# Cross attention and a sorted mixture of experts on one core: first masks in six pieces, tails cleared earlier and in larger blocks, fewer waits for landings

## The reference, cut to what matters

```python
# x (16, 100, 128), ctx (16, 1444, 128), mask (16, 1444)
x = x + tanh(g_xattn) * xattn(layernorm(x), ctx, mask)      # one head, softmax over 1444 keys
#   att = q . w_input + (q * dot_scale) @ ctx.T - 1e30 * mask ; softmax(att) @ ctx
x = x + tanh(g_ffn) * moe(layernorm(x))                      # 8 experts, top 2 of 8
#   per token and expert: W_down @ (silu(W_gate @ t) * (W_up @ t)), F = 512, weighted by the gates
```

## Time and profile before

| what | value |
|---|---|
| runs before | 282.87 us median of 3 (278.66, 322.13, 282.87) |
| profiled execution | 280.85 us, span 278.8 us, mean granted clock 0.946 |
| PE busy | 242.4 us of 278.8 (87%) |
| DVE, ACT, POOL busy | 144.4, 137.0, 112.2 us |
| attention, 16 batches | from 12.4 us to about 152 us |
| first expert tile / tile 8 / last down | gate and up at 148.2 / 184.5 / 257.7 us |
| last reads, additions and stores | 262.7 to 278 us |

### The profile page before, as it was taken

One profiled execution on the slowest core, in us unless ns is written; L12 is line 12 of the kernel. 1 busy time (PEld: TensorE's weight loads), 2 busy tenths in 40 slices (PEclk: granted clock), 3 DMA queues, 4 the chain that ended last, 5 costly groups with the idle time before them and its releaser, 6 DMA issues.

```text
span 278.8 us, 5798 instructions
## 1 busy us (share of the span) xinstructions
PE 242.4 (87%) x1614; PEld 198.3 (71%) x1615; DVE 144.4 (52%) x467; ACT 137.0 (49%) x302; POOL 112.2 (40%) x197
## 2 busy tenths in 40 slices
PE   6799999999999999999978599699999999998100
PEld 6557777788777788777778387588888888887100
DVE  3434666767777767787746338223433343432024
ACT  3445455676555686655545234345545555545000
POOL 3250432157644476636374535433424223233200
PEclk9989999999999999999979979989999999999855
DMA  5875787778787888888632003221211111000164
GB/s 134 223 199 149 186 218 195 187 210 228 200 244 210 214 191 207 206 218 225 246 76 49 15 2 91 63 70 58 58 39 45 54 38 38 28 19 31 34 218 119
DMA packets 17645, 36.49 MB, mean 131 GB/s; under 512 B 3692, under 2 KB 9460, under 8 KB 17620
## 3 DMA queue, kind: packets, MB, share of 16 engines
q1 hardware_dynamic: 13580, 31.36, 43.4%
q0 software_dynamic: 2560, 3.77, 4.5%
q10 hardware_dynamic: 1480, 1.05, 1.2%
HBM read 30.89 MB, written 5.27 MB: 130 GB/s over the span
## 4 chain that ended last, share of the span: by engine, by line
PE 70%; DMA 8%; issue 6%; DVE 5%; ACT 4%; POOL 4%; SPq 0%; POOLq 0%; DVEq 0%; ACTq 0%
PE psum L1067 14%; PE psum L1046 13%; PE psum L1170 9%; PE psum L1022 7%; PE psum L1148 6%; PE psum L1150 5%; PE psum L1149 5%; PE psum L1159 4%; DMA ctx_sb<-results 3%; PE psum L1057 2%; DMA slots<-pair_rows,slot_i 2%; ACT probsT L616 2%; POOL slots L527 2%; DMA results<-y_sb,dest 2%; ACT qT L611 1%
## 5 line engine op out<-in xcount | busy, mean ns | idle before, releaser
L583 POOL DMA_INDIRECT results<-y_sb,dest x32 | 30.7, 959 | 57.1 <-DVE dest L948 25.6
L1067 PE MATMUL psum<-ctx_sb,probsT 120*100 120x128 f32 (+1 forms) x384 | 49.2, 280 | 0.0
L959 DVE SCALAR_TENSOR_TENSOR scores<-probs,row_in,psum 128x512 f32<-128x512 f32 x32 | 23.9, 747 | 42.6 <-ACT probs L691 41.3
L1067 PEld LDWEIGHTS psum<-ctx_sb,probsT 120*100 120x100 f32 (+1 forms) x384 | 44.9, 172 | 0.3 <-issue 0.2
L1046 PE MATMUL psum<-ctxT,qT 128*100 128x512 f32 (+1 forms) x96 | 43.2, 587 | 0.0
L527 POOL DMA_INDIRECT slots<-pair_rows,slot_i x32 | 33.5, 1046 | 22.6 <-DVE slot_i L846 8.4
L691 ACT ACTIVATE probs<-psum 128x512 f32<-128x512 f32 x32 | 19.1, 598 | 39.0 <-PE psum L1150 39.0
L1170 PE MATMUL psum<-w_down,hidT 128*128 x256 | 34.3, 277 | 0.8 <-ACT y_sb L706 0.6
L782 DVE CUSTOM_DVE_ANT_0 scores<-psum,maskb 100x1444 f32<-100x1444 f32 x16 | 26.6, 1660 | 13.3 <-PE psum L1046 13.3
L1170 PEld LDWEIGHTS psum<-w_down,hidT 128*128 128x128 f32 x256 | 31.5, 194 | 1.2 <-issue 1.2
L1148 PE MATMUL psum<-w_hi,rowT_hi 128*128 x64 | 29.1, 454 | 2.4 <-issue 1.0
(11 more groups left out here) (138 smaller groups left out, 372.2 us busy)
## 6 DMA issues: line engine op xcount, KB each, us to landing
ctx_sb<-in_ctx SPq DMA_DIRECT2D x16, 720.0 KB
maskb<-mask_scaled SPq DMA_DIRECT2D x14, 564.1 KB
w_raw<-in_w_experts SPq DMA_DIRECT2D x16, 256.0 KB, 6.0
row_in<-slots SPq DMA_DIRECT2D x32, 65.0 KB, 1.9
w_down<-in_w_experts SPq DMA_DIRECT2D x4, 512.0 KB, 9.2
ctx_sb<-results SPq DMA_DIRECT2D x4, 200.0 KB
ctx_sb<-results ACTq DMA_DIRECT2D x4, 200.0 KB
out<-x_all SPq DMA_DIRECT2D x4, 200.0 KB
```

The costliest lines, as they stand in the source:

```text
L583: nc.gpsimd.indirect_dma_start(results, bass.IndirectOffsetOnAxis(ap=dest[:, s:s + 1], axis=0), y_sb[:, s, :], None).then_inc(y_stored[s], 16)
L1067: last = nc.tensor.matmul(attn_ps[0:Q, 0:D], probsT[0:rows[c], c, :], ctx_sb[0:rows[c], b % RING, c, :], start=(c == 0), stop=(c == CHUNKS ...
```

## The change

The changes, by place:

- **First masks.** The mask is padded to 1536 keys and laid as 48 pieces of 512. One transfer brings the first 32 pieces and a second one pieces 0 to 5 again, into rows 32 to 37; one ACT instruction of 38 x 512 and one DVE instruction of 6 x 512 take the place of the 16 x 1444 ones. `add_mask` is three matmuls, not six, and that of batch 0 moves ahead of `transpose_q(0)`. The scaling and the storing of the masks move behind the eviction of the first context, and `load_ctx(3)` behind the wait for that store. Tanh moves behind the first exponential. Seven of the 17 filler matmuls go (`keep_warm`: 10, 3 and 4 become 10 and 2, with the third call gone).
- **Attention.** `transpose_q(b+1)` and `copy_qT(b+1)` move behind the transposed context, PE's behind the first third of `attend`, ACT's ahead of the exponential.
- **End of attention.** The routing of batch 13 moves out of `step(15)` to behind it; orders on PE, ACT and DVE change for the last three batches; `transpose_rows(8)` moves to the end of step 7; the late tables are spread over tiles 3 to 6 on DVE.
- **Tails.** `tail_row` is written in `place(6)`, when 14 batches are counted. SP clears 328 rows behind that point for each of the 8 experts, each with one transfer of 82 partitions x 4 rows (82 x 2080 bytes). SP's row load of tile 8 does not wait for them; instead POOL waits for all of them before it scatters batches 14 and 15.
- **Waits of POOL.** Late scatters are `scatter(11)`, root2(14), wait, `scatter(12)`, root2(15), `scatter(13)`, last gates, wait for tails, `scatter(14)`, `scatter(15)`. `scatter_result` waits for no landing.

```diff
+TAIL_ROWS = 328
+TAIL_PART = 82
-        empty = sb("empty", [P, ROW])
+        empty = sb("empty", [P, SPREAD, ROW])          # SPREAD = TAIL_ROWS // TAIL_PART = 4
...
             load_x(0)
-            sp.dma_start(mask_rows, mask).then_inc(mask_raw, 16)
+            sp.dma_start(first_raw[0:LOW, :], pieces[0:LOW, :]).then_inc(first_loaded_mask, 16)
+            sp.dma_start(first_raw[LOW:first_rows, :], pieces[0:MASKED * PIECES, :]).then_inc(first_loaded_mask, 16)
             load_ctx(0)
             load_x(1)
+            sp.dma_start(mask_rows, mask[:, 0:K]).then_inc(mask_raw, 16)
             load_ctx(1)
...
                 if k == EARLY:
                     sp.wait_ge(late_ready, 1)
-                    sp.wait_ge(tails_stored, 16 * E)
                     sp.wait_ge(empty_stored, 16)
                     sp.wait_ge(scattered[1], 16 * 2 * (B - PARTS[EARLY_PART][1]))
...
             def clear_tail(e):
-                at = sp.value_load(tail_row[0:1, e:e + 1], min_val=0, max_val=DUMMY)
-                sp.dma_start(slots[bass.ds(at, P), :], empty[:, :]).then_inc(tails_stored, 16)
+                at = sp.value_load(tail_row[0:1, e:e + 1], min_val=0, max_val=DUMMY - TAIL_ROWS)
+                sp.dma_start(slots[bass.ds(at, TAIL_ROWS), :].rearrange("(p r) d -> p r d", r=SPREAD),
+                             empty[0:TAIL_PART, :, :]).then_inc(tails_stored, 16)
...
                 if n == EARLY - 1:
                     sp.wait_ge(tails_ready, 1)
-                    for e in range(SP_TAILS):
+                    for e in range(E):
                         clear_tail(e)
...
-            pair_landed(1)
-            scatter(12)
+            scatter(11)
             root2(B - 2)
             normalise2(B - 2)
             pair_landed(1)
-            scatter(13)
+            scatter(12)
             root2(B - 1)
             normalise2(B - 1)
+            scatter(13)
             last_gates()
-            pair_landed(1)
+            pool.wait_ge(tails_stored, 16 * E)
             scatter(14)
-            pair_landed(1)
             scatter(15)
-            pair_landed(1)
...
                 pool.wait_ge(dest_done, n + 1)
-                if k % 2 == 0:
-                    wait(pool, y_stored[(k - 1) % YRING], i * 16 + 16 * ((k + YRING - 1) // YRING) if k else 0)
                 apart(pool)
...
             def step(b):                                # ACT
-                if 0 <= b - 1 < B:
-                    if b + 1 < B:
-                        act.wait_ge(probsT_raw, (b - 1) * GROUPS + 1)
-                        copy_qT(b + 1)
+                if b >= 1:
                     for g in range(GROUPS):
                         copy_probsT(b - 1, g)
...
-                if 0 <= b - 2 < B - 2:
+                if 0 <= b - 2 < B - 3:
                     copy_xn2T(b - 2)
+                if b + 1 < B:
+                    copy_qT(b + 1)
...
                 dve.wait_ge(rank_raw, p + 1)            # DVE, place(p)
+                if p == LAST - 1:
+                    nc.vector.tensor_copy(tail_row[:, :], at[:, N, :]).then_inc(tails_ready, 1)
                 if p == LAST:
-                    nc.vector.tensor_copy(tail_row[:, :], at[:, N, :]).then_inc(tails_ready, 1)
...
             def between(n):                             # DVE, after tile n
                 if n == 3:
+                    tile_counts(True)
+                if n == 4:
                     tile_runs(True)
-                if n == 4:
-                    tile_tables(True)
+                if n == 5:
+                    tile_experts(True)
+                if n == 6:
+                    tile_rows(True)
...
-                for n in range(0, K, 512):              # PE, add_mask(b)
-                    m = min(512, K - n)
-                    nc.tensor.matmul(scores_ps[0:Q, n:n + m], select[:, b, :], mask_hi[:, n:n + m], start=True, stop=False)
-                    nc.tensor.matmul(scores_ps[0:Q, n:n + m], select[:, b, :], mask_lo[:, n:n + m], start=False, stop=False)
+                for t, n in enumerate(range(0, K, PIECE)):
+                    m = min(PIECE, K - n)
+                    nc.tensor.matmul(scores_ps[0:Q, n:n + m], select[:, b * PIECES + t, :], first_split[:, 0:m], start=True, stop=False)
...
-                if b == 0:                              # PE, step(b)
-                    keep_warm(4)
                 if 4 <= b and b % 2 == 0:
                     ranks((b - 4) // 2)
...
+                if 2 <= b < B - 1:
+                    transpose_xn2(b - 2)
+                if b >= 1:
                     attend(b - 1, 0, 1)
+                if b + 1 < B:
+                    transpose_q(b + 1)
...
-                if 0 < k and k + 1 < T:                 # PE, tile_step
+                if 0 < k and k + 1 < T and k != EARLY - 1:
                     transpose_rows(i, k + 1)
...
+                if k == EARLY - 1:
+                    transpose_rows(i, k + 1)
                 if k == 2:
+                    route(B - 1)
                     pe.wait_ge(x2_done, B)
                     pe.wait_ge(down_loaded, 16 * 4)
```

More of the change, by code:

```diff
@@ L78, in build @@
     CUTS = 4
+    PIECES = 3
+    PIECE = mask.shape[1] // PIECES
+    LOW = 32
+    assert PIECE == 512 and K <= PIECES * PIECE and MASKED * PIECES <= LOW
+    SPREAD = TAIL_ROWS // TAIL_PART
+    assert TAIL_ROWS >= (TOKENS - PARTS[-2][1] * Q) + P - 1 and PARTS[-2][1] * Q + TAIL_ROWS <= REGION
     CUT = B // CUTS
@@ L366, in _ @@
             load_ctx(2)
-            load_ctx(RING - 1)
             sp.wait_ge(mask_stored, 16)
             load_mask(MASKED)
+            load_ctx(RING - 1)
             load_x(3)
@@ L381, in _ @@
                     sp.wait_ge(empty_done, 1)
-                    sp.dma_start(slots[DUMMY:DUMMY + P, :], empty[:, :]).then_inc(empty_stored, 16)
+                    sp.dma_start(slots[DUMMY:DUMMY + P, :], empty[:, 0, :]).then_inc(empty_stored, 16)
             for m in range(4):
@@ L546, in _ @@
             for b in range(B):
+                if b == B - 1:
+                    pair_landed(0)
+                    scatter(b - 5)
                 if b >= 2:
@@ L660, in _ @@
             nc.scalar.activation(warm[:, :], wi_col[:, :], ACT.Exp)
+            act.wait_ge(first_loaded_mask, 32)
+            nc.scalar.activation(first_split, first_raw, ACT.Copy, scale=NEG).then_inc(mask_hi_done, 1)
+            copy_qT(0)
+            evict_ctxT(0, 0)
+            evict_ctxT(0, 1)
             act.wait_ge(mask_raw, 16)
@@ L706, in tile_step @@
                     nc.scalar.activation(y_sb[:, s, :], y_ps, ACT.Copy).then_inc(y_done, 1)
[L708 to L715 removed]
             rowT_high(0, 0, first_rowT_ps)
[L717 removed]
+            copy_xn2T(B - 3)
             for g in range(GROUPS):
                 copy_probsT(B - 1, g)
[L720 removed]
+            exp_gap(LAST - 1)
+            nc.scalar.activation(warm[:, :], wi_col[:, :], ACT.Silu)
+            rowT_high(0, 1)
+            over_tiles(act, tile_step)
             act.wait_ge(attn_raw, B)
@@ L876, in tile_tables, with tile_rows @@
                 link(nc.vector.tensor_scalar(tile_expert[:, t0:t0 + nt], tile_sum[:, 0:nt], float(E - 1), None, ALU.min))
+            def tile_rows(late):
+                nt = LATE if late else EARLY
+                t0 = EARLY if late else 0
                 link(nc.vector.tensor_tensor(moved[:, 0:nt, :], reached[:, 0:nt, :],
@@ L923, in _ @@
             apart(dve)
-            nc.vector.tensor_tensor(mask_lo, mask_rows, mask_hi.bitcast(F32), ALU.subtract).then_inc(mask_lo_done, 1)
+            nc.vector.scalar_tensor_tensor(out=first_split[LOW:first_rows, :], in0=first_raw[LOW:first_rows, :], scalar=NEG,
+                                           in1=first_split[LOW:first_rows, :].bitcast(F32), op0=ALU.mult,
+                                           op1=ALU.subtract).then_inc(mask_lo_done, 1)
             dve.wait_ge(scale_loaded, 32)
@@ L941, in tile_step @@
                 n = i * YRING + k
-                if 0 < k and k + 1 < T:
+                if 0 < k and k + 1 < T and k != EARLY - 1:
                     rowT_low(i, k + 1)
@@ L981, in _ @@
             residual(B - 2)
+            statistics2(B - 2)
+            attention_gain(B - 1)
             rowT_low(0, 0, first_rowT_ps)
-            statistics2(B - 2)
+            top_two(B - 3)
+            choose(LAST - 1)
+            place(LAST - 1)
             gate_pair(LAST - 1)
-            place(LAST - 1)
-            attention_gain(B - 1)
+            rowT_low(0, 1)
             over_tiles(dve, tile_step, between)
@@ L1003, in transpose_q @@
                 pe.wait_ge(xn_done, b + 1)
+                wait(pe, ctxT_act, 2 * b + 1 if b else 0)
                 nc.tensor.transpose(ring_ps[0][:, GROUP * Q:GROUP * Q + Q], xn[:, b % 2, :],
@@ L1048, in score, with transpose_probs @@
                 last.then_inc(scores_raw, 1)
-            def transpose_probs(b, q_too):
+            def transpose_probs(b):
```

(4 more changed lines are left out.)

116 lines of the change are left out of this document (46 added, 70 removed).

## The result

| | before | after |
|---|---|---|
| runs | 281.19 us median of 4 (278.66 to 322.13) | 291.24 us median of 4 (289.44 to 292.82) |
| profiled execution, span, clock | 280.85, 278.8, 0.946 | 289.44, 287.7, 0.934 |
| scores of batches 0, 1, 15 | 12.36, 20.92, 136.51 | 13.06, 20.90, 135.12 |
| first clear issued | 166.56 | 147.48 |
| gate and up of tiles 0, 7, 8, 31 | 148.16, 180.10, 184.54, 252.03 | 143.41, 170.69, 192.76, 261.29 |

The ratio is 1.0433, with a 95% interval of 1.0325 to 1.0541: **slower**. It compares fast runs alone; of the kernel before these are 278.66 and 279.52, and the other two were over 1.5% above the fastest. The forecast was 282, no change; 291.24 lies within its range of 272 to 292, near the upper end. The wait for the tails came by the mechanism that was forecast and cost 10.4 us where 8.8 were forecast; what was to be won against it at the start was not won.

The account below looks back on a forecast made before the run. PE was taken to bound the kernel, busy 87% of the span. From the profiled 280.85 us, less 4.7 (start), 2.0 (steady attention) and 1.2 (results), plus 8.8 (tails), came 281.8, rounded to 282 us; range 272 to 292.

Parts of the forecast that it names:

- The sum: Whole kernel: the profiled execution less three gains plus one loss, 280.85 - 4.7 - 2.0 - 1.2 + 8.8 = 281.8 us.
- Start: Up to batch 1's scores: earlier mask, full clock, fewer fillers and fewer mask matmuls were to win 4.7 us.
- I take it as gone: Scores of batch 0: the 1.6 us lost to the lower clock after idle PE was to vanish.
- `load_ctx(3)` and the stored masks move later; they are needed two batches on: Start: moving the fourth context load and the mask store later was to cost nothing.
- Steady attention: PE's wait before the context transposes was to shrink by 0.15 us in each of 13 batches, winning 2.0 us.
- Results: End of the kernel: the last result's scatter, no longer held for a landing, was to win 1.2 us.
- Tails: Clears on two DMA engines were to hold POOL's scatters of batches 14 and 15; tile 8 starts 8.8 us later.
- 8 x 3.8 = 30.2 us: Eight clears queue at 3.8 us each, 41 pieces of 92 ns on each of two engines.
- The two rivals about the clears: Clears spread over all engines, 263.6 us, chance 0.12; or clears split into 520-byte rows, 311 us, chance 0.05.
- 263.6: Total in us if clears spread over all engines, with 9.3 won between 135 and 190 us; chance 0.12.
- the 520-byte pieces: Slow-side rival: clears split into rows of 520 bytes, 59 us for all, total 311 us; chance 0.05.
- its own case's 0.76: Chance of the forecast's main case, range 277 to 290 us: 0.09 below, 0.53 within, 0.14 above no change.

Follow-up runs that it names:

- ctx3_82: The changed kernel, clears still on 82 partitions, with `load_ctx(3)` issued ahead of SP's wait for the mask store; 288.85 us, ratio 1.0310 to the kernel before.
- warm_8: The changed kernel with `keep_warm(8)` instead of `keep_warm(2)` ahead of the first context transposes; 292.08 us, ratio 1.0456 to the kernel before.
- ctx3_warm: The changed kernel with clears on 112 partitions, `load_ctx(3)` ahead of the mask-store wait and `keep_warm(8)` instead of `keep_warm(2)`; 270.11 us, ratio 0.9685 to the kernel before.
- experiment 1: The changed kernel with clears on 112, 87 or 83 partitions instead of 82; 276.05 (271.38 on another chip), 283.94 and 320.51 us.
- ctx3_early: The changed kernel with clears on 112 partitions and `load_ctx(3)` ahead of SP's wait for the mask store; 269.39 us, ratio 0.9671 to the kernel before.
- tables_5: The changed kernel with 112-partition clears, early `load_ctx(3)` and the late tables in three tile steps instead of four; 268.03 us, ratio 0.9560 to the kernel before.

## Why the prediction was wrong, by its own steps

**The sum.** Forecast on the profiled execution 281.8, measured 289.44: 7.6 us more. Tile 8's gate and up were forecast at 193.3 - 4.7 - 2.0 = 186.6 and came at 192.76. The row loads began at 137.43 instead of 139.57 - 6.7 = 132.9, 4.6 late: 4.7 that the start did not win and 0.6 of the attention, less 0.7 won behind batch 15. The clears then came 1.1 later still, released by `tail_row` at 146.74, behind the last row load (137.43 + 8.68 = 146.11). The eight took 31.3 us from first data (147.48 + 0.8 = 148.3) to the last landing at 179.60, where the forecast had 30.2 + 0.4: 0.7. POOL began 0.9 behind that landing and not 0.1: 0.8. From POOL's start to the rows 9.5 and not 9.9, then 2.8 and not 3.4 to tile 8: 1.0 back. 4.6 + 1.1 + 0.7 + 0.8 - 1.0 = 6.2. Behind it 1.0 for tile 8 itself, whose period is 3.89 us at half clock and not 2.82, and 0.75 for the results; the time outside the span is 0.3 shorter. Together 7.65. So 4.6 of the miss are gains that did not come before the row loads, and 2.6 are the tails.

**Start: this step failed.** "Sum 1.8 + 1.6 + 1.0 + 0.3 = 4.7 us" won 0.0 at batch 1 (20.92 before, 20.90 after). Two parts of it were wrong. "The two new small loads [...] delay it by one issue, 0.35 us; the context was waited for by nothing, so that is hidden": that is misread. The context was complete at 7.90 in the trace of before and PE's first weight load for it began at 7.94, so it was the last input already and left no room. In the changed kernel it was complete at 9.31, 1.41 us later for 0.35 us of later issue, and PE waited; in the other twelve profiles with the new order it was 9.12 to 10.35. The other was "I take it as gone, since PE's gap shrinks to about 1 us". PE's gap before the scores did shrink to 1.04, yet the scores of batch 0 ran at least in part at half clock in 10 of the 11 profiles with the new order and `keep_warm(2)`, and at full clock in both with `keep_warm(8)`. The half clock cost 2.2 us in the scores and 1.3 in the transposes, which before had run at full clock (1.41 us). It does not follow that the removed fillers had kept the clock: five of the 17 go (not seven, as stands ahead), four of them behind the scores of batch 0, at 18.46, and only one ahead of the context, and with all of them the scores took 4.28 us in the kernel before, mostly at half clock too. What `keep_warm(8)` shows is that more fillers than either kernel has hold it there. Where the clock was back by 11.2 (`ctx3_82`) 2.7 of the 4.7 were won, and the other 2.0 are the scores at 12.62 and not at 10.6. That more small transfers ahead of the context made it late is argued from 93 instead of 160 GB/s; no run moved them. Nor is it shown why, of the eleven, the clock came back by 11.2 in `ctx3_82` alone.

**"`load_ctx(3)` and the stored masks move later; they are needed two batches on"** was costed at nothing. In the shipped kernel PE waited 0.3 us in all for contexts between 26 and 127 us, so the time does bear it out. But the slack was small: in `warm_8`, where PE came 3.3 us earlier, it waited 3.93 us for context 4, complete at 40.85; in `ctx3_warm`, with the fourth load early, that context was complete at 37.88 and the wait was 1.0.

**Steady attention: mechanism right, size a little over.** The waits before the context transposes fell from 0.31 to 0.16 us, as forecast, and the periods by 0.25 and 0.16. Net 1.4 of the 2.0 arrived at batch 15: PE waited once for ACT's copy of the normalised rows (0.33 us at 67.49) and once for POOL's rows (0.49 us at 123.81), and the periods in which these waits fall, from batch 6 to 7 and from 13 to 14, were 0.6 and 0.75 us too long.

**Results: mechanism right, size off.** 0.45 us, not 1.2. Between the copy and a scatter that waits for nothing lie 1.06 us, not 0.3: the lower bound, 0.5, was the right value.

**Tails: mechanism right, size low.** Two engines, 0.13, POOL idle until the clears are in, PE idle 17.2 us, half clock behind it. "8.8 us later" measured 10.4, taken from the first row load to tile 8 (55.3 us, 45.0 before), and 1.0 more for tile 8 itself. "8 x 3.8 = 30.2 us" measured 31.3, of which the last three clears took 3.6 each and the first five 4.1. The two rivals about the clears are refuted: spread over all engines, it would have been the kernel of experiment 1 (276 or 271, not 263.6), and the trace has 656 packets of 2080 bytes for the clears, 8 x 82, and so no pieces of 520 bytes. That 263.6 was too good has the same cause as the miss: it too had the 4.7 in it.

**The sign.** The forecast "no change" was a gain of 7.9 against a loss of 8.8. The loss was read from the traffic of many similar transfers; the larger part of the gain hung on a clock level that was taken as gone without a row for it, and on a landing that was taken as early. The rival on the slow side should have been that one, with the whole 4.7 us lost (the bound "if the lower clock stays, 3.0 us is left" covered only the clock), and not the 520-byte pieces. That the measured time still falls within the range is owed to its width, which allowed for slower clears: 0.14 of its own case's 0.76 lay above 288.5.

## What to carry to other kernels

The number of partitions of a transfer is a speed setting: take one with the divisor 16 (here 112 for 82, 15 to 20 us), above all where an in-order engine waits for the whole group before work that others need. Filler matmuls ahead of a gap can be worth their time: here 16 in place of 4 brought batch 1 3.3 us forward. Judge them by the durations behind them, and look whether the next wait takes the gain back, as it did here. When a load that nobody waits for is moved behind a wait, its landing time, not the time it is asked for, has to be priced; and when one stall goes, read what is late next (here the table on DVE) before the version is called done.

## What the runs showed of the hardware that was not expected

- Clears with 1, 2 and 3 engines ran at 24, 46 and 68 GB/s: one engine writes 23 to 24 GB/s in 2080-byte pieces (88 ns a piece at the end of each group) whether or not others run, and from 1 to 3 engines the rate grows in proportion.
- After 17.2 us without a matmul, PE was at half clock from 178.0 to 195.1, that is for 5 us after it had begun again; after 2.27 us (`ctx3_early`) from 170.3 to 173.7, and in `tables_5`, where the gap before tile 8 is 0.58 us and the longest from 18 to 245 us is 1.09, not at all.
- In all fourteen profiles PE's first weight load of the context transposes begins 0.04 to 0.05 us behind the landing of the first context, also where the timeline shows no wait (7.94 behind 7.90 in the kernel before).
- The same kernel with 112 partitions took 276.05 us on one chip and 271.38 on another, with idle stretches of ACT of 2.55 and 3.64 us in the slower profile that the trace puts down to nothing on the core. Their cause stays open.
